# GpSimd's tile loop of layer 1: 32 looped turns against 43 turns written out with constant index columns

## The reference, cut to what matters

```
xn = layernorm(x);  x = x + attention_0(xn) + experts_0(xn)     # top 1 of 8, 128 -> 512 -> 128
xn = layernorm(x);  x = x + attention_1(xn) + experts_1(xn)     # top 2 of 8
# experts_1, for each token and each of its two experts e, weighted by a softmax over the two logits:
z = (xn @ W1[e] + b1[e]) * (xn @ W2[e] + b2[e])                 # 128 -> 256
g = z @ Wg[e] + bg[e]                                           # 256 -> 256
o = g * sigmoid(g) * (z @ Wl[e] + bl[e])                        # 256 -> 256
y = o @ W3[e] + b3[e]                                           # 256 -> 128
```

## Time and profile before

| | us |
|---|---|
| median of 3 runs | 497.09 (494.24 to 498.85) |
| the profiled execution | 493.56 |
| its span, first to last instruction | 491.4 |
| TensorE busy | 382.9 (78% of the span) |
| VectorE busy | 249.4 (51%) |
| GpSimd busy | 225.1 (46%) |
| ScalarE busy | 169.4 (34%) |

### The profile page before, as it was taken

One profiled execution on the slowest core, in us unless ns is written; L12 is line 12 of the kernel. 1 busy time (PEld: TensorE's weight loads), 2 busy tenths in 40 slices (PEclk: granted clock), 3 DMA queues, 4 the chain that ended last, 5 costly groups with the idle time before them and its releaser, 6 DMA issues.

```text
span 491.4 us, 9938 instructions
## 1 busy us (share of the span) xinstructions
PE 382.9 (78%) x2683; PEld 335.1 (68%) x2704; DVE 249.4 (51%) x791; ACT 169.4 (34%) x455; POOL 225.1 (46%) x341
## 2 busy tenths in 40 slices
PE   2877788999989989965329967899988988897900
PEld 0666677978878877855317635789988888887800
DVE  5347967757567664100183799534433343333323
ACT  1523333434434334432106222144433433433312
POOL 9346617074374361665413011235555666555422
PEclk9999899999999999989759998899999999999965
DMA  8730000000000000532212061058877776777254
GB/s 282 238 109 0 2 1 2 1 0 1 2 0 2 1 21 13 183 118 91 85 39 87 1 204 54 26 176 277 260 248 235 231 232 217 237 230 219 59 149 123
DMA packets 35261, 54.74 MB, mean 111 GB/s; under 512 B 4096, under 2 KB 21824, under 8 KB 35232
## 3 DMA queue, kind: packets, MB, share of 16 engines
q1 hardware_dynamic: 31392, 46.12, 30.4%
q0 software_dynamic: 3840, 8.26, 5.4%
HBM read 46.57 MB, written 7.80 MB: 111 GB/s over the span
## 4 chain that ended last, share of the span: by engine, by line
POOL 26%; issue 24%; PE 24%; DVE 13%; DMA 7%; ACT 2%; POOLq 2%; SPq 1%; DVEq 1%; ACTq 0%
POOL xg L543 6%; POOL y_rows L558 6%; POOL shared L488 5%; POOL shared L484 4%; PE bank L1232 4%; DMA xg<-xn_rows,ig 3%; PE bank L845 2%; PE bank L985 2%; PE bank L947 2%; PE bank L1220 1%; POOL ig L540 1%; POOL isc L555 1%; PE bank L969 1%; DMA xnT<-y_rows 1%; PE bank L1174 1%
## 5 line engine op out<-in xcount | busy, mean ns | idle before, releaser
L1232 PE MATMUL bank<-kf,shared 128*128 128x128 f32 x624 | 76.8, 277 | 0.0
L1232 PEld LDWEIGHTS bank<-kf,shared 128*128 128x128 f32 x624 | 72.7, 192 | 0.2
L558 POOL DMA_INDIRECT y_rows<-ysb,isc x40 | 39.9, 997 | 32.7 <-POOL isc L555 29.4
L1423 DVE TENSOR_REDUCE rmax<-bank 128x8 f32<-128x512 f32 (+2 forms) x48 | 30.2, 629 | 47.8 <-PE bank L947 25.0
L985 PEld LDWEIGHTS bank<-shared 128*128 128x128 f32 x344 | 45.3, 195 | 13.2 <-issue 11.3
L543 POOL DMA_INDIRECT xg<-xn_rows,ig x40 | 39.6, 991 | 31.6 <-POOL ig L540 20.6
L985 PE MATMUL bank<-shared 128*128 128x128 f32 x344 | 47.7, 281 | 6.4 <-DVE remn L1463 6.4
L1669 DVE SCALAR_TENSOR_TENSOR aT<-bank,bcol,at 128x128 f32<-128x128 f32 x78 | 23.8, 346 | 57.1 <-ACT at L824 54.3
L845 PE MATMUL bank<-cb 128*128 128x512 bf16 x90 | 27.7, 436 | 27.5 <-DVEq L1278 16.5
L1220 PE MATMUL bank<-xtT,shared 128*128 128x128 f32 x312 | 42.2, 279 | 1.4 <-ACT xtT L817 0.9
L824 ACT ACTIVATE at<-bank,bcol 128x128 f32<-128x128 f32 x78 | 24.4, 363 | 52.2 <-PE bank L1232 52.2
(11 more groups left out here) (233 smaller groups left out, 738.8 us busy)
## 6 DMA issues: line engine op xcount, KB each, us to landing
shared<-in_w1s SPq DMA_DIRECT2D x39, 512.0 KB, 4.0
shared<-in_w1s SPq DMA_DIRECT2D x39, 256.0 KB, 3.8
we<-in_we SPq DMA_DIRECT2D x8, 514.0 KB, 3.4
xn_rows<-xn SPq DMA_DIRECT2D x8, 256.0 KB, 2.6
xn<-y_rows SPq DMA_DIRECT2D x8, 256.0 KB, 3.9
x<-in_x SPq DMA_DIRECT2D x4, 256.0 KB, 3.4
y_rows<-qe POOLq DMA_DIRECT2D x4, 256.0 KB, 5.6
w1s<-in_w1s SPq DMA_DIRECT2D x2, 512.0 KB, 8.2
```

The source lines that it names most:

```text
L558: pool.indirect_dma_start(out=dst, in_=ysb[:, slot_b, :], in_offset=None, out_offset=bass.IndirectOffsetOnAxis(ap=index.bitcast(U32), axis ...
L1232: mm = pe.matmul(bank[(1, 3)[(k - 1) % 2]][:, P * f:P * f + P], wglb[:, (k - 1) % 4, 2 * F1 * a + P * f:2 * F1 * a + P * f + P], zT2[:, (k ...
L1423: dve.tensor_reduce(rmax[:, g % 2, :], s3, X, ALU.max).then_inc(s_max, 1)
```

## The change

GpSimd's tile turns of layer 1 no longer go through `tile_turns`. A Python loop calls the same `tile` for all 43 turns with q = 0 and `single` true, so that every turn is written out, and every tile number is a constant:

```
-            tile_turns(pool, tile)
+            for k in range(J1 + 4):
+                tile(0, k, True)
```

## The result

The changed kernel takes 508.95 us (median of 4 runs, 507.91 to 510.54) against 497.0 us before (494.24 to 498.85): ratio 1.0248, 95% interval 1.0192 to 1.0304. It is slower by 12 us, where I had forecast 481 us, 16 us faster. The profiled execution after is 510.54 us, its span 508.7 us.

A forecast was written before the change was run, and what follows sets the result against it. GpSimd was taken to bound layer 1's tile turns at 3.99 us; with it at 2.5 us, TensorE would set 3.37 us, gaining 16.0 us over 26 tiles: 497.1 - 16.0 = 481 us, own range 477 to 484.5, full range 476 to 487.5.

The forecast's parts named there:

- That GpSimd sets the pace: Layer 1's looped tile turns: GpSimd has no slack and takes 3.99 us from gather to gather, matching TensorE's 3.985 a tile.
- GpSimd's turn written out: Layer 1's tile turns: two transfers and two 0.30 us gaps make 2.5 us, 1.5 us less than the 3.99 before.
- the sum: Whole kernel: median 497.1 us minus 16.0 us gained gives 481 us; this forecast had chance 0.76.
- TensorE's turn: Layer 1 from tile 12 on: TensorE sets the pace at 3.37 us instead of 3.985 a tile, gaining 16.0 us.
- The last sign of being wrong: Last of the listed observations that would refute the forecast: TensorE's own turns lengthen.
- The gathers' spare time: Gathers behind scatters that wait for y: still 3.0 to 4.4 us early, so the moved wait costs nothing.
- the weights: Weight transfers in the tile turns: DMA share rises to 89%, cost taken as nothing, upper bound 0.25 us a tile, 6 us.
- the clock: TensorE goes from 87% to about 99% busy; granted clock stays 1.00, 2.4 GHz, so matmuls keep their durations.
- the tail: End of the kernel, last scatters: moves forward as a whole and gives no gain of its own.
- The longer program: 28 more turns' bodies written out on GpSimd: no fetch cost taken, up to 0.8 us a turn absorbable.
- The rivals: Transfers become the bound, 487 us, chance 0.11; gathers stay late, 487 to 497 us, 0.06; slower code fetching, 513 us, 0.03.
- The slower one: Rival: GpSimd stalls fetching written-out code; at 2 us a turn the pace is 4.5 us, time 513 us; chance 0.03.

The follow-up runs named there:

- Experiment 5: Changed kernel with a 128 x 512 memset on GpSimd ahead of each gather and scatter, gaps of 0.7 us: 481.67 us, ratio 0.9708.
- experiment 1: Changed kernel, all turns written out, but the 32 formerly looped turns copy their index column and wait as before: 498.4 us, ratio 1.0017.
- experiment 6: Changed kernel with 128 x 832 memsets ahead of each gather and scatter, gaps of about 1.0 us: 496.21 us, ratio 0.9983.
- experiment 11: Kernel with 0.7 us gaps in layer 1, with layer 0's nine expert turns written out and spaced by memsets too: 480.26 us, ratio 0.9696.
- experiment 2: Kernel before, still looped, each looped turn making both copies first, then gather and scatter 0.3 us apart: 486.78 us, ratio 0.9791.
- experiment 7: Changed kernel with one 128 x 832 memset per turn, ahead of the gather: 489.56 us, ratio 0.988.
- experiment 8: Changed kernel with one 128 x 832 memset per turn, ahead of the scatter: 490.21 us, ratio 0.987.

## Why the prediction was wrong

**That GpSimd sets the pace** at 3.99 us: right. Experiment 5 makes its turn shorter and gains the forecast time.

**GpSimd's turn written out** at 2.5 us: right where nothing is waited for, 0.97 us for a transfer and 0.30 between two. But a scatter that waits for ysb starts 0.82 us after VectorE has it (348.68 less 347.58 + 0.28, in the rows above), where I had put 0.30 in the check on the gathers. That takes 0.5 us of their 3.0 to 4.4 us of spare time and doesn't touch the sum.

**TensorE's turn, the step that failed.** I wrote that since 2.5 is under 3.37, TensorE sets the pace from tile 12 on. TensorE's pace of 3.37 us came from tiles 4 to 12, in which GpSimd's issues were still 1.0 us apart. I took it as a property of TensorE alone and carried it into a state in which they are 0.30 us apart. There the pace was 4.24. Where the issues are 0.70 us apart it is 3.38 us a tile, tile 38 starts at 448.6, 87.8 us after tile 12, and the time is 481.67 us, the number forecast. The sum was right, for a kernel that keeps its transfers apart. The last sign of being wrong that I had named, TensorE's own turns getting longer, is the one that came.

**How a late increment becomes a long turn.** This is read from the rows from 342 to 350 us above. TensorE works on, as its own stream doesn't need the value. ScalarE's silu (L825), which waits for L1233, starts 2.3 us late, and ScalarE works in order, so the h2 behind it (L812), which waits for the L1221 of 344.31, is late as well. VectorE's kf and ysb follow, and TensorE waits at L1242 and L1221: from the L1221 of 344.31 to that of 349.75 it is 5.4 us. GpSimd meanwhile waits 3.5 us for ysb, after which two tiles' scatters and gathers are ready at once, so it issues four transfers in a row, and the next increment is late. So the burst makes the delay, and the delay makes the next burst. That fits its going on in nearly every second turn, and gaps of 0.49 us being no better than 0.30; it is read from the timelines, and no run tested this loop by itself.

**The gathers' spare time, the weights, the clock, the tail**: right for experiment 5. TensorE has no wait for gathers or weights there. I had worked out a DMA share of 89% and it is 0.89; the granted clock is 1.00, 2.4 GHz; from TensorE's start on W1 and W2 of tile 38 to the end it is 31.2 us, before 30.6. The Trainium skill, DMA: Bandwidth & Descriptors, section "Latency and other measured facts", gives 2 us of HBM latency at high load; at a share of 0.89 TensorE waited for no gather, and the latency itself no run here shows. In the changed kernel the clock did not stay up: it was at its lower level, 1.2 GHz, in part of the turns that start at 375.63, 436.49 and 453.89 us, each after turns in which TensorE had waited. Such a turn took 4.9 to 5.0 us in place of 3.3, but the next one was as much shorter than usual (the two took 8.5 to 8.8 us, ordinary pairs of turns 8.5 to 8.9), so the clock explains none of the 12 us.

**The longer program** at nothing: right, by experiment 1.

**The rivals.** None was it. The slower one came out on the right side and near the right size, 4.5 us a tile and 513 us, but by luck: experiment 1 excludes its mechanism, and I gave it 0.03. What the profile could have told me: the earlier trace rows has transfers 0.30 us apart only where TensorE had few increments on which others waited (two fell into such issues from 320 us on). I treated a rare state as one whose price the rows had shown. The copies were dead weight by the names of their operands, but in the timeline they and their waits were also the only thing between two issues; taking away a pause that another resource may be using is a cost to bound, and my range had no bound for it.

What stays open: why the issue of a second transfer holds up another engine's increments. The trace doesn't say either whether the increment itself is held up or the last write of the matmul ahead of it. Recorded completions of transfers were scarce in the same stretch too (one from 344.8 to 346.0 us, then 27 in 1 us), though the DMA engines moved 227 GB/s there (a share of 0.64), and VectorE's and ScalarE's increments were on time. That could point to something that TensorE and the DMA engines share. But it is not shown: the changed kernel's trace holds 2,475 records of completions where that of the kernel before holds 4,054, so a record that is missing may be a record that was lost.

## What to carry to other kernels

When an engine that is the bound gets faster, its work doesn't only end earlier, it also gets denser; take the next engine's pace from a stretch in which the first was already that dense, or bound the difference. If a wait has no named releaser, compare two engines that wait for the same semaphore with the instruction that increments it: if both start late together, the increment is late. On GpSimd, issue indirect transfers at even distances rather than as fast as possible: here 0.54 us of idle work ahead of each was worth 27 us. This is one kernel; elsewhere the distance that is enough has to be measured.

## What the hardware showed unexpectedly

- Indirect transfers issued by GpSimd 0.30 to 0.63 us apart made TensorE's semaphore increments up to 2.4 us late; where all of them were 0.70 us or more apart, 0 of 347 increments were late by more than 0.2 us (experiments 5, 6 and 11).
- The number of rows that the scatters move did not matter for this: with 16 rows instead of 128 a scatter's issue took 0.86 instead of 0.98 us, and increments were as late.
- The pace was 0.15 to 0.44 us a tile over 3.37 with runs of two (experiments 2, 7 and 8), and about 0.9 us over it with runs of four.
- A scatter that had waited for VectorE started 0.82 us after VectorE's end, one that waited for nothing 0.30 us after the transfer before it.
- Written-out code on GpSimd, 32 turns instead of four in a loop, cost nothing measurable: ratio 1.0017 (0.9976 to 1.0057).
